# GpSimd's gathers of expert outputs, each held back until one more expert step is done

## What is computed

```python
probs = jax.nn.softmax(xf @ gate_w, axis=-1)
dispatch_w, expert_idx = jax.lax.top_k(probs, 2)
combine = jnp.sum(one_hot(expert_idx, 8) * dispatch_w[..., None], axis=1)
for e in range(8):
    h = jax.nn.gelu(xf @ w1[e] + b1[e], approximate=False)      # 128 -> 512
    y = h @ w2[e] + b2[e]                                       # 512 -> 128
    out = out + combine[:, e:e + 1] * y
```

## Time and profile before

| | us |
|---|---|
| timed runs of the kernel, median of 3 | 424.3 (423.45 to 424.38) |
| the profiled execution, span from the first to the last instruction | 446.6 |
| TensorE busy in that span | 386.1 |
| VectorE busy | 296.5 |
| ScalarE busy | 218.7 |
| GpSimd busy | 134.1 |

### The profile page before, as it was taken

How to read it: one execution, slowest core, us unless ns; L and a number is a source line. 1 busy time by engine, 2 the same in 40 slices (tenths; PEclk the granted TensorE clock), 3 DMA queues, 4 the chain that set the end, 5 groups by cost and what they waited for, 6 DMA issues and landing times.

```text
span 446.6 us, 9131 instructions
## 1 busy us (share of the span) xinstructions
PE 386.1 (86%) x2864; PEld 304.2 (68%) x2864; DVE 296.5 (66%) x947; ACT 218.7 (49%) x460; POOL 134.1 (30%) x139
## 2 busy tenths in 40 slices
PE   2572869998999999999999999999999999349975
PEld 2341758584568965688545895589999998349865
DVE  1477997889999779886899868972277331026205
ACT  1227484934892345422463237954376574126512
POOL 6771044133222411022458102520013005700270
PEclk9997788999999999999999999999999999559999
DMA  5899500000000000000029221010000323111211
GB/s 158 323 376 426 216 1 1 1 1 0 1 1 1 1 1 1 1 1 2 12 88 325 84 60 45 24 48 1 4 0 31 97 79 102 53 35 43 84 53 53
DMA packets 24021, 31.71 MB, mean 71 GB/s; under 512 B 4377, under 2 KB 18720, under 8 KB 22696
## 3 DMA queue, kind: packets, MB, share of 16 engines
q1 hardware_dynamic: 21416, 25.62, 16.5%
q0 software_dynamic: 2560, 5.52, 4.1%
HBM read 18.15 MB, written 12.98 MB: 70 GB/s over the span
## 4 chain that ended last, share of the span: by engine, by line
PE 64%; DVE 12%; ACT 6%; another core or an unknown queue 6%; issue 5%; POOL 3%; DMA 2%; DVEq 0%; ACTq 0%; POOLq 0%
PE bank L1063 8%; PE bank L1052 7%; PE bank L926 5%; PE bank L939 4%; PE bank L955 4%; PE bank L978 3%; PE bank L971 3%; PE bank L963 3%; PE bank L893 2%; PE bank L873 2%; PE bank L911 2%; PE bank L1015 2%; PE bank L887 2%; PE bank L920 2%
## 5 line engine op out<-in xcount | busy, mean ns | idle before, releaser
L1268 ACT ACTIVATE arena<-bank,arena 128x128 f32<-128x128 f32 x168 | 47.5, 369 | 50.5 <-PE bank L1052 27.9
L1063 PE MATMUL bank<-big,arena 128*128 x336 | 47.3, 287 | 16.1 <-DVE h L1620 7.5
L1063 PEld LDWEIGHTS bank<-big,arena 128*128 128x128 f32 x336 | 43.1, 201 | 17.5 <-issue 17.3
L718 POOL DMA_INDIRECT dealt<-xy,arena x28 | 30.0, 1073 | 40.0 <-DVE arena L1655 32.7
L1714 DVE COPY w1s<-big 128x512 f32 x42 | 17.8, 425 | 36.5 <-PE bank L1052 14.6
L926 PE MATMUL bank<-xT_f,wq 128*128 128x512 f32 x64 | 29.0, 595 | 0.5 <-DVE lb L1532 0.5
L734 POOL DMA_INDIRECT vv<-experts_out,arena x16 | 15.1, 943 | 32.9 <-issue 32.9
L1546 DVE TENSOR_TENSOR arena<-bank,causal 128x512 f32<-128x512 f32 x32 | 20.3, 681 | 4.0 <-PE bank L939 4.0
L926 PEld LDWEIGHTS bank<-xT_f,wq 128*128 128x128 f32 x64 | 11.8, 190 | 14.9 <-issue 13.4
L1052 PE MATMUL bank<-arena,w1s 128*128 128x128 f32 x160 | 21.1, 276 | 0.0
L1078 ACT ACT_TABLE_LOAD x16 | 20.5, 1283 | 1.1 <-PEq L1811 0.8
(11 more groups left out here) (283 smaller groups left out, 989.8 us busy)
## 6 DMA issues: line engine op xcount, KB each, us to landing
dealt<-lb SPq DMA_DIRECT2D x7, 1024.0 KB, 13.4
big<-in_tv SPq DMA_DIRECT2D x2, 2048.0 KB
big<-in_ew SPq DMA_DIRECT2D x16, 256.0 KB, 3.1
arena<-dealt SPq DMA_DIRECT2D x20, 64.0 KB, 1.8
experts_out<-arena SPq DMA_DIRECT2D x5, 256.0 KB, 2.6
wq<-in_wq SPq DMA_DIRECT2D x1, 1024.0 KB, 17.7
out<-h SPq DMA_DIRECT2D x4, 256.0 KB
fs<-dealt SPq DMA_DIRECT2D x8, 64.0 KB, 1.9
```

The source lines that it names most:

```text
L718: pool.indirect_dma_start(xs[b // LEAD], bass.IndirectOffsetOnAxis(ap=goal[b][:, k, t:t + 1], axis=0), xy[b % 2][:, t, :], None).then_inc( ...
L1063: last = pe.matmul(p[:, 0:D], hid[n % 2][:, c * P:(c + 1) * P], big[:, bass.ds(e * FF + (E * FF + c * D), D)], start=(c == 0), stop=(c == ...
L1268: last = act.activation(hid[n % 2][:, c * P:(c + 1) * P], of("K.up", n)[:, c * P:(c + 1) * P], ACT.Gelu, bias=eb1[:].rearrange("p e c -> p ...
```

## The change

GpSimd gets one more wait ahead of each gather of section Y. With i = 2 at + k, where `at` is the tile within the group and k the first or second expert of the token: in group 0 gather i (0 to 15) waits for the down multiplication of expert tile 26 + i. In group 1 (i = 0 to 11) the gather of the first expert waits for the first gelu of dense expert 2 + at, and that of the second for the down multiplication of dense expert 1 + at. In VectorE's order Y0.1 moves from behind K34.4 to behind J2.3, and Y1.1 from behind K38.4 to behind J3.3.

```diff
-        "K31.4 K32.4 K36.0 K37.0 K38.0 K33.4 K34.4 Y0.1 K39.0 K35.4 K36.4 K37.4 K40.0 K41.0 K38.4 Y1.1 K39.4 "
-        "K40.4 K41.4 J2.3 J3.3 J4.3 J5.3 Y2.1 J6.3 Y3.1 J7.3"),
+        "K31.4 K32.4 K36.0 K37.0 K38.0 K33.4 K34.4 K39.0 K35.4 K36.4 K37.4 K40.0 K41.0 K38.4 K39.4 "
+        "K40.4 K41.4 J2.3 Y0.1 J3.3 Y1.1 J4.3 J5.3 Y2.1 J6.3 Y3.1 J7.3"),
...
                     for t in range(PART[b]):
                         for k in range(2):
                             at = b % LEAD * T + t
+                            i = 2 * at + k
+                            if g == 0:
+                                wait(pool, "K.pe2.down", len(OF_TILE) - 4 * T + i)
+                            elif k == 0:
+                                wait(pool, "J.act.ht0", LEAD + i // 2)
+                            else:
+                                wait(pool, "J.pe2.down", LEAD + i // 2 - 1)
                             pool.indirect_dma_start(
                                 yg[b][:, k, t, :], None, ys[g],
                                 bass.IndirectOffsetOnAxis(ap=posi[g][:, k, at:at + 1], axis=0)).then_inc(s_yg[b], 16)
```

## The result

On the chip of the first comparison the changed kernel takes 426.01 us (425.42 to 427.37, 6 runs) and the kernel before 424.34 (423.45 to 424.63, 6 runs). The ratio is 1.0055, with a 95% interval from 1.0036 to 1.0074. The time forecast was 426.3 us.

A forecast was written before the change was run, and what follows sets the result against it. TensorE was taken to bound the kernel, its stops beside gathers mostly an effect of profiling. Moves and tile waits cost 0, the last gather's lateness 2.0 us: 424.3 + 2.0 = 426.3 us, range 421.5 to 428.3.

The forecast's parts named there:

- The dense stage's term: Last gather waits for J6.2, so the end moves from T + 0.7 to T + 2.6 (T: J7.2's end); 2.0 us taken.
- one wait more than said: Nine of twelve dense-stage waits and three of sixteen before were to be past when GpSimd reaches them.
- What was costed at nothing: Tile-stage waits, group 1's start and the moved combinations: cost 0 each, at worst some tenths for the move.
- the moved combinations: Y0.1 and Y1.1, 2.68 us each on VectorE, fit beside its dense-stage work: cost 0, at worst some tenths.
- group 1's start: Group 1's gathers start when they did, since group 0's last gather is issued while GpSimd waits for group 1's stores: cost 0.
- the waits in the tile stage: Group 0's gathers go at one per 1.79 us after the first three, rather than per 1.25: cost 0.
- The step that failed: TensorE's stops beside the gathers, 24.6 us in the profile, belong mostly to the profiled execution, not to timed runs.
- The arithmetic: Profiled span less stops is 422.0 us against the timed median of 424.3, leaving room for about 2.3 us of stops.
- The supporting argument: Four scatters from 337.91 us on lie beside unbroken TensorE work, so an indirect transfer as such does not stop it.
- the stops are partly real: Rival: ordinary executions also stop while gathers are issued, so the change gains up to 5.5 us, to 420.8 us; chance 0.22.
- The two rules: By SBUF's rule spacing gathers gives TensorE nothing; by NOTIFIC's the stops would be wholly the recording's.

The follow-up runs named there:

- e4: The kernel before with Y0.1 and Y1.1 moved behind J2.3 and J3.3 and no waits added: 453.7 us against 453.2, ratio 1.0033.
- e1: The kernel before, run again without any edit on another chip than the first: median 451.84 us.
- e8b: The kernel before with each gather replaced by a plain load of 128 consecutive rows: 425.79 us against 453.79 for the kernel before.
- e3: The kernel before with the dense stage's waits alone, combinations left in the tile stage: 446.1 us against 453.2, ratio 0.9869.
- e2: The changed kernel without its dense-stage waits, tile waits and moved combinations kept: 437.3 us against 453.2 for the kernel before, ratio 0.9676.
- e7b: The changed kernel with the tile stage's gathers released in fours: 440.08 us, against 433.0 for the changed kernel on that chip.
- f2: The kernel before with Y0.1 and Y1.1 moved and a GpSimd write ahead of each group 0 gather, no waits: 434.5 us against 451.7.

## Why the prediction was right on one chip, and wrong beyond it

**The dense stage's term** was right in mechanism and in its first figure: the last gather was to start at T - 1.5 and started at T - 1.51, held by J6.2 as said (1.20 us of idle, released by TensorE). From there the end was to come at T + 2.6; it came at T + 2.97. The mis-sized part is the latency from the gather's start to VectorE's: 2.57 us (416.52 to 419.09), where the data's 1.9 us and an estimate of 0.2 for the rest gave 2.1. Measured by the tail, the loss is 2.3 us, against 2.0 taken and 1.7 between the medians (ratio 1.0055, that is 1.5 to 3.1 us). Two slips changed nothing: one wait more than said bound anything (the ninth gather, i = 8, was held for 0.44 us), and of TensorE's row in the page the last two slices are under 9, not three.

**What was costed at nothing** was nothing that could be told: the moved combinations (e4), group 1's start, and the waits in the tile stage on a chip without stops, where that stage took 24.8 us, 0.2 more than with plain loads.

**The step that failed** is the paragraph on the stops: that they "are mostly a matter of the profiled execution" and "cannot be 20 us in the timed ones". The arithmetic was right for the runs it was made with, and they indeed had no room for stops. The conclusion from it was not: timed runs of the same kernel take 452 us and have the stops. The prediction took one profile and three times for two views of the same state, when they were of two. The supporting argument, that the scatters lie beside unbroken TensorE work, read only TensorE's matmuls and not its signals, which come 2.3 us late there. That the time came out as forecast is in part luck, for the comparison ran in the state of the three timed runs and not in that of the profile, and nothing in the working could tell which it would be. What is left of the idea is that the stops may belong to the recording. Timed runs come with a span and a clock too, those of the changed kernel at 426 us as well as those of before at 452, so recording alone does not bring them; but the recordings are not alike, and in those with stops most landing records of the gathers are missing. The rival "the stops are partly real" was priced at up to 5.5 us and given 0.22; where stops exist at all they are about 24 us (24.5: e1's 42.2 + 28.3 against the first chip's 24.8 + 21.2), and the changed kernel removes most of them. On those chips the time of 433.0 us lies outside the range in its figure, though far below its own before.

**The two rules.** By the Trainium skill, SBUF — State Buffer ("SBUF: two separate sides"), transfers cannot slow TensorE. Plain loads agree with it (e8b). The indirect gathers do not: TensorE stood still for up to 15 us beside them (e1, e3). The measurement decides, and the rule does not cover whatever the indirect form does besides moving bytes. By the Trainium skill, NOTIFIC — the notification-queue block ("Overflow: three behaviours, one of which stalls the engine"), a full path of records would hold TensorE up, and it would do so rather than lose a record inside. Holding up fits late signals and matmuls that come apart, and a store that fills fits the start of the stop in e2's dense stage, after five gathers, and the cost of bursts (e7b). That landing records are missing in the same traces does not fit the second half of the rule, unless they are lost elsewhere. No run here shows that the stops are this; if they are, something else that differs between the chips must decide whether the store fills.

**What stays open.** Why one chip has no stops and two have them; what it is in an indirect transfer, as against a plain load, that holds TensorE's signals back; and whether the missing records are a cause, an effect or a neighbour. Whether the stops exist in an execution of which nothing is recorded can't be seen from here, since every time of the experiments comes with a record. If they do not, the change would lose its 2 us everywhere outside a recording.

## What to carry to other kernels

When a profile's span and the timed runs differ by more than what lies around a span (here 22 us against 1.8), find out whether they are the same state before either is explained: run the kernel unchanged again, on another chip too. Where an engine stands still for something that the profile can't name, compare the start of the instruction that needs a result with the end of the one that made it: an unbroken row of matmuls does not say that their results were announced. Indirect gathers issued back to back beside a busy TensorE can stop it in recorded executions, and here a step of 1.65 us or more removed most of that; padding did it as well as waits. Let the last of them be due a full latency (here 2.5 to 3.1 us, and the combination's 1.4) ahead of the last matmul, or the cure costs 2 us where there is nothing to cure.

## What the runs showed of the hardware that was not expected

- One kernel, without an edit, takes 424 us in one comparison and 452 us on two other chips, with ranges of 423.5 to 424.6 and 447 to 457 us; 24.5 us of that are in the two stages with gathers (e1 against the changed kernel on the first chip).
- Eight matmuls of one up multiplication can be spread over 3 us with no wait in the program (e1).
- A result of TensorE was announced up to 16.9 us after its recorded end beside gathers (e1), and 2.3 us beside four scatters (before); on the first chip it took 0.01 to 0.02 us.
- An indirect gather of 128 rows of 512 bytes holds GpSimd for 0.94 us with 0.30 us to the next; a plain load of the same bytes takes 0.54 with none. From the last indirect gather's start to the first use of its data pass 2.57 us on the first chip and 2.48 to 3.09 on the others.
- A write of 128x512 by GpSimd, 0.52 us alone at the program's start, took 0.54 to 0.79 us between gathers (f2).
